# Values of the first self attention made for all heads at once, 512 columns at a time, and kept in the output buffer

## The chip, the core and the metric

The kernel runs on one core of a Trainium2 chip. The core has the engines TensorE (PE), VectorE (DVE), ScalarE (ACT) and GpSimd (POOL), and SyncE (SP), which issues the DMAs here. Each works through its own queue in order, and semaphores tie the queues together. SBUF holds the data, and PSUM, in eight banks of 128 partitions x 512 float32, takes what TensorE writes. The metric is the device time of one execution in microseconds (us).

## The reference, cut to what matters

Two decoder blocks run one after the other on x of shape (2, 1024, 256). The change touches only the first self attention of block 0 and the layer norm ahead of it:

```python
h = _layernorm(x, ln1_g, ln1_b)                # (2, 1024, 256)
q = (h @ wq).reshape(B, S, 16, 64)             # wq, wk, wv: 256 x 1024
k = (h @ wk).reshape(B, S, 16, 64)
v = (h @ wv).reshape(B, S, 16, 64)
attn = softmax(einsum('bihd,bjhd->bhij', q, k) * 64 ** -0.5)
out = einsum('bhij,bjhd->bihd', attn, v).reshape(B, S, 1024)
x = out @ wo + bo + x
```

All of it is float32. Cross attention, the gated feed forward layer and the whole of block 1 follow; they take the rest of the time and aren't touched.

## The kernel before

**Norm stage.** `project_norm` with the name ln01 normalises x in 9 groups of one or two tiles of 128 tokens. For each group DVE takes the statistics (`stats_of`) and ACT the root, DVE scales (`normalise`), PE transposes (`turn`), and ACT writes the transposed rows to hT, 128 partitions x 2 x 2048 (`evacuate`). A `Beside` object lets other work run in the slots of that loop; before the change only the split of the first weights into a coarse and a remaining part (`w_hi`, `w_lo`) runs there.

**Attention.** `wide_attention` handles two heads at a time (g = 0 to 7) for each of the two batches b: 16 bodies, `both(g, b)`. The code gives the first two bodies and the last two unrolled; the others are a hardware loop. A body has 8 units of two steps each. In a step, ACT seeds a score bank with the negative row maxima (`seed`), PE adds three products of the hi and lo parts of keys and queries (`scores`), ACT takes the exponential to `p_buf` (`exponent`), POOL adds `p_buf` up for the denominators, and PE multiplies `p_buf` with the values in `v_buf` (`weighted`).

Beside it each body prepares the next one, in "front items": the projections k and q of 512 tokens (6 matmuls each; ACT takes the hi part out of PSUM and DVE the lo part), the values v, sixteen m items (two products each for the row maxima, reduced by DVE), t (the transposed maxima, which DVE negates and SP sends through DRAM to `m_all`, from where the seeds come) and den (denominators). The tables `lanes` and `lanes_first` say in which unit of a body each item stands. In a unit PE does the items up to the first m (`leading`), the two steps of scores, the remaining items (`trailing`), and then the weighted products of the unit before. `first_front` is the list of items ahead of the first body, for which nothing else runs: I call this stretch the front.

All front items share three PSUM banks (`NBANK = 3`). An item takes the bank of its place in the `lanes` table, modulo 3 (an m item takes two places), whichever body it stands in, and PE's `wait_free` waits until the last user of that bank has been drained; for an m item it waits for both banks before the first product.

**Values before.** For each (g, b), items ("v", 0) and ("v", 1) each make the values of 512 tokens for the two heads at hand: 4 token tiles x 2 halves of the contraction, eight float32 matmuls of 128 columns (L1032), which PE runs as 16 passes; DVE copies the bank to `v_buf` (L1239). The weights `wv` of two heads are loaded for each g.

## Time and profile before

| | us |
|---|---|
| median of 3 runs | 1852.04 (1851.66 to 1856.6) |
| the profiled execution, device time | 1845.68 |
| its span, first to last instruction | 1844.0 |
| PE busy in the span | 1683.9 (91%) |
| DVE, ACT, POOL busy | 1179.0, 1057.4, 955.7 |
| const and norm stage, until the attention starts | 0 to 31.7 |
| front, until the first scores | 31.7 to 68.9 |
| first body, until the second body's scores | 68.9 to 127.4 |
| the other 15 bodies | 127.4 to about 786 |

The profile gives busy times by engine, and tables by line, by stretch and in order of time. "Idle before" an instruction is what its engine waited, with the engine that released it. Busy times of overlapping matmuls are not additive; what one costs is read from start to start.

### The profile page before, as it was taken

How to read it: one execution, taken by the hardware profiler on the slowest of the kernel's cores; microseconds unless marked ns; L12 is line 12 of the kernel's file. 1: busy time of each engine (PE TensorE's matmuls, PEld its weight loads, DVE VectorE, ACT ScalarE, POOL GpSimd, SP SyncE). 2: the span in 40 equal slices, each digit the busy share in tenths (PEclk: the TensorE clock that was granted, in tenths of full speed). 3: DMA queues.
4: the chain of work that ended last, by engine and by line, in shares of the span. 5: the costliest groups of instructions: out<-in, count | busy, mean ns of one | idle time of the engine just before them, and what ended most of it. 6: DMA issues, size and time to landing. Idle time of an engine off the chain costs nothing. (4 is left out here: it accounts for less than half of the span.)

```text
span 1844.0 us, 29564 instructions
## 1 busy us (share of the span) xinstructions
PE 1683.9 (91%) x10028; PEld 1079.8 (59%) x10028; DVE 1179.0 (64%) x2043; ACT 1057.4 (57%) x1389; POOL 955.7 (52%) x732
## 2 busy tenths in 40 slices
PE   4689999999999999988999889996989887998799
PEld 2345555555555555477666778884444436655679
DVE  5567777777776777475776843347787745787513
ACT  3367777787877787843555432311676673444452
POOL 1268888888888788951222620201334443566205
PEclk9899999999999999998999999996999999999899
DMA  2000100000000000030000010102334321000001
GB/s 83 18 26 30 36 32 26 29 26 29 26 29 26 29 26 24 24 103 27 1 1 1 13 32 23 30 12 62 76 71 105 72 71 30 10 1 7 26 17 47
DMA packets 53810, 62.46 MB, mean 34 GB/s; under 512 B 18064, under 2 KB 43820, under 8 KB 53711
## 3 DMA queue, kind: packets, MB, share of 16 engines
q1 hardware_dynamic: 53711, 61.16, 12.0%
q8 instruction: 60, 0.98, 0.2%
q14 instruction: 39, 0.32, 0.1%
HBM read 41.72 MB, written 2.37 MB: 24 GB/s over the span
## 5 line engine op out<-in xcount | busy, mean ns | idle before, releaser
L1336 POOL TENSOR_TENSOR x<-x,sa_p_buf 128x1024 f32<-128x1024 f32 x190 | 452.3, 2381 | 122.7 <-ACT sa_p_buf L1153 110.2
L1245 DVE TENSOR_REDUCE sa_mx<-sa_front 128x1 f32<-128x512 f32 x512 | 328.3, 683 | 113.3 <-PE sa_front L1041 112.3
L1153 ACT ACTIVATE sa_p_buf<-sa_score 128x1024 f32<-128x1024 f32 x256 | 248.9, 1023 | 130.2 <-PE sa_score L1078 130.2
L1093 PE MATMUL sa_out<-sa_p_buf,sa_v_buf 128*64 128x512 f32 x1024 | 246.2, 602 | 0.0
L607 ACT ACTIVATE sa_p_buf<-sa_score 128x1024 f32<-128x1024 f32 (+1 forms) x160 | 140.6, 943 | 76.0 <-PE sa_score L555 75.8
L402 DVE TENSOR_REDUCE sa_mx<-sa_front 128x1 f32<-128x512 f32 (+1 forms) x224 | 136.5, 651 | 31.5 <-PE sa_front L316 27.8
L1911 POOL TENSOR_TENSOR x<-x,bias_out 128x1024 f32<-128x1024 f32 x24 | 60.5, 2534 | 165.0 <-POOLq L2233 142.9
L1778 POOL TENSOR_TENSOR ca_probs<-ca_s_sb,ca_inv 128x616 f32<-128x616 f32 x64 | 78.0, 1219 | 120.5 <-DVE ca_inv L1694 120.5
L1093 PEld LDWEIGHTS sa_out<-sa_p_buf,sa_v_buf 128*64 128x64 f32 x1024 | 64.8, 136 | 120.2 <-issue 92.3
L1163 ACT ACTIVATE sa_score<-sa_m_all 128x1024 f32<-128x1024 f32 x128 | 130.7, 1033 | 6.1 <-DMA sa_m_all<-sa_m_line 6.1
L1041 PE MATMUL sa_front<-sa_k_hi,sa_q_hi 64*128 64x512 f32 x512 | 118.2, 458 | 12.4 <-DVE sa_mx L1245 6.6
L1163 ACT ACTIVATE sa_score<-x 128x1024 f32<-128x1024 f32 x128 | 127.8, 1031 | 2.6 <-DMA x<-sa_m_line 2.6
L660 POOL TENSOR_SCALAR_AFFINE_SELECT sa_p_buf<-sa_p_buf 128x128 f32<-128x128 f32 x256 | 65.7, 295 | 120.5 <-ACT sa_p_buf L607 120.5
L1267 DVE RECIPROCAL x<-x 128x128 f32<-128x128 f32 x124 | 108.7, 920 | 18.5 <-ACT x L1176 18.3
L1041 PEld LDWEIGHTS sa_front<-sa_k_hi,sa_q_hi 64*128 64x128 f32 x512 | 48.4, 185 | 113.1 <-DVE sa_mx L1245 38.2
L1601 ACT ACTIVATE ca_turned<-ca_t_ps 128x1024 f32<-128x1024 f32 x64 | 65.5, 1024 | 74.1 <-PE ca_t_ps L1547 74.1
L1078 PE MATMUL sa_score<-sa_q_hi,sa_k_hi 64*128 64x512 f32 x512 | 105.4, 408 | 2.7 <-ACT sa_score L1163 2.6
L1078 PE MATMUL sa_score<-sa_q_hi,sa_k_lo 64*128 64x512 f32 x512 | 101.1, 391 | 0.0
L1078 PE MATMUL sa_score<-sa_q_lo,sa_k_hi 64*128 64x512 f32 x512 | 100.7, 390 | 0.0
L1336 POOL TENSOR_TENSOR x<-sa_p_buf 128x1024 f32<-128x1024 f32 x32 | 75.9, 2372 | 46.2 <-ACT sa_p_buf L1153 46.2
L316 PE MATMUL sa_front<-sa_k_top,sa_q_top 33*128 33x128 f32 (+4 forms) x504 | 71.3, 349 | 23.8 <-DVE sa_mx L402 14.8
L316 PEld LDWEIGHTS sa_front<-sa_k_top,sa_q_top 33*128 33x128 f32 (+1 forms) x504 | 43.7, 193 | 78.0 <-DVE sa_mx L402 52.9
(238 smaller groups left out, 3587.9 us busy)
## 6 DMA issues: line engine op xcount, KB each, us to landing
sa_m_all<-sa_m_line SPq DMA_DIRECT2D x16, 512.0 KB, 3.6
x<-sa_m_line SPq DMA_DIRECT2D x16, 512.0 KB, 3.6
x<-in_x SPq DMA_DIRECT2D x8, 512.0 KB, 6.6
sa_q_stack<-sa_hi SPq DMA_DIRECT2D x32, 128.0 KB, 2.6
sa_k_stack<-sa_hi SPq DMA_DIRECT2D x32, 128.0 KB, 2.7
sa_recip<-sa_den_out SPq DMA_DIRECT2D x32, 128.0 KB, 2.6
ff_w<-in_L_xattn_ff_w SPq DMA_DIRECT2D x16, 128.0 KB, 2.2
sa_k_top<-sa_hi SPq DMA_DIRECT2D x32, 64.0 KB, 2.3
```

The costliest lines, as they stand in the source:

```text
L316: mm = pe.matmul(bank(i, item, u)[:, c0 + lo_k:c0 + hi_k], q_top[base:base + rows_of, b, r, at], k_top[base:base + rows_of, b, r, k0 + lo_ ...
L402: dve.tensor_reduce(mx[:, b, j, place:place + 1], fr[u][:, 0:n], AX.X, ALU.max).then_inc(drained, 1)
L607: nc.scalar.activation(p_buf[:, n % NPB, 2 * r:2 * r + 2, 0:cols], score_ps[r][:, :, 0:cols], ACT.Exp, scale=SCALE).then_inc(exp_done, 1)
L1041: pe.matmul(front_ps[bank(item, j)][:], q_hi[r, b, qt * P:(qt + 1) * P], k_hi[r, b, half * HALF:(half + 1) * HALF], start=True, stop=True) ...
L1078: mm = pe.matmul(score_ps[s % len(score_ps)][:, j, :], ks[r, b, keys], qs[r, b, queries], start=False, stop=(part == 2), skip_group_check= ...
L1093: mm = pe.matmul(out_ps[64 * j:64 * j + 64, :], v_buf[:, b, kt, 64 * j:64 * j + 64], p_buf[:, s % NPB, j, :], start=(kt == 0), stop=(kt == ...
L1153: nc.scalar.activation(p_buf[:, s % NPB], score_ps[s % len(score_ps)][:], ACT.Exp, scale=SCALE).then_inc(exp_done, G)
L1163: nc.scalar.activation(score_ps[s % len(score_ps)][:], m_all[h].rearrange("p (j n) -> p j n", j=G), ACT.Identity).then_inc(seeded, G)
L1245: dve.tensor_reduce(mx[:, b, j, qt, half:half + 1], front_ps[bank(item, j)][:], AX.X, ALU.max).then_inc(drained, 1)
L1267: dve.reciprocal(recip[:, h, at], recip[:, h, at]).then_inc(inverted, 1)
L1336: nc.gpsimd.tensor_tensor(acc[:, h], prev, cur, ALU.add).then_inc(added, 1)
L1778: nc.gpsimd.tensor_tensor(probs[:, n % 2, :, 0:TC], s_sb[:, n % NS], inv[:, n % 2, :].unsqueeze(2).to_broadcast((P, U, TC)), ALU.mult).the ...
```

## The change

The values of all sixteen heads are made once. Item n of 32 multiplies one tile of 128 tokens with 512 columns of wv, the columns of eight heads: two float32 matmuls of 512 columns. The result goes to the output buffer oT, into the places that the attention's own output takes later, and for each (g, b) one DMA brings 1024 columns of it to `v_buf`.

- Items 0 to 7 run in the norm stage (`AHEAD = 8`), in three PSUM banks of their own, one in each slot from 2 on; ACT takes them out.
- Items 8 to 17 (`IN_FRONT = 10`) run in the front, in the idle score banks, ACT takes them out.
- Items 18 to 31 stand in `lanes_first`, at the ends of the units of the first body (1, 1, 2, 2, 2, 2, 2, 2 of them), in the three front banks; DVE copies them (14 copies).
- The tables lose ("v", 0) and ("v", 1); q1 moves from unit 3 to 4, and in `first_front` behind t. A body has 40 places in place of 42.
- The front no longer primes the score banks with four products (L1101): the items 8 to 17 write them.
- All of wv, 1 MB, is loaded in the const stage, to the memory of the output weights `w_out`, whose own load moves from the start of the front to the second body. The loads of wq and wk for the first heads move from the norm stage to the const stage.
- The split of hT (`split_rows` on ACT, `rest_of_rows`) for batch 0 moves from the front into the norm stage, slots 4 and 6, with the lo part on POOL where DVE did it; that for batch 1 stands behind k1 in the front.
- In this norm stage, DVE takes the statistics of group i + 1 ahead of normalising group i.

```diff
+    def values(self, pe, n, ps):
+        half, tile = divmod(n, TT)
+        if n == 0:
+            pe.wait_ge(self.wv_in, DMA)
+        for k in range(KD):
+            mm = pe.matmul(ps, self.hT[:, k, tile * P:(tile + 1) * P], self.wv[:, k, half * HALF:(half + 1) * HALF],
+                           start=(k == 0), stop=(k == KD - 1))
+        return mm
...
+    def keep_values(self, act, n, ps):
+        act.wait_ge(self.v_full, n + 1)
+        self.nc.scalar.activation(self.values_to(n), ps.rearrange("p (g d) -> p g d", d=P),
+                                  ACT.Identity).then_inc(self.v_made, 1)
...
+    def tensor(self, pe, slot, ready):
+        n = slot - 2
+        if 0 <= n < self.AHEAD:
+            ready(n // GROUP)
+            if n >= len(self.early_ps):
+                pe.wait_ge(self.v_made, n - len(self.early_ps) + 1)
+            self.values(pe, n, self.early_ps[n % len(self.early_ps)][:]).then_inc(self.v_full, 1)
...
-        3: [("n", ("m", 2, 0)), ("n", ("m", 3, 0)), ("n", ("q", 1))],
-        4: [("n", ("m", 0, 1)), ("n", ("m", 1, 1)), ("n", ("v", 0))],
+        3: [("n", ("m", 2, 0)), ("n", ("m", 3, 0))],
+        4: [("n", ("m", 0, 1)), ("n", ("m", 1, 1)), ("n", ("q", 1))],
...
-        7: [("n", ("m", 6, 0)), ("n", ("m", 7, 0)), ("n", ("v", 1)), ("n", ("m", 4, 1))],
+        7: [("n", ("m", 6, 0)), ("n", ("m", 7, 0)), ("n", ("m", 4, 1))],
...
+    for u, count in enumerate((1, 1, 2, 2, 2, 2, 2, 2)):
+        lanes_first[u] = lanes_first[u] + [("c", ("v", n)) for n in in_lanes[:count]]
+        in_lanes = in_lanes[count:]
...
-    assert NSLOT % NBANK == 0
...
+                def load_values(g, b):
+                    sp.dma_start(v_buf[:, b], value_cols(g, b)).then_inc(v_in, DMA)
...
+                    if is_first(g, b):
+                        sp.wait_ge(v_made, TT)
+                    else:
+                        sp.wait_ge(pv_done, lin(g, b, STEPS, 0))
+                    load_values(g2, b2)
                     maxima(g2, b2, 0)
...
-                for c in range(HALVES, CHUNKS):
-                    pool.wait_ge(h_high, c + 1)
...
+                    first_w.rest_of_rows(pool, c)
...
+                if not KN:
+                    stats_of(0)
                 for i in range(NG):
-                    stats_of(i)
+                    if KN:
+                        stats_of(i)
+                    elif i + 1 < NG:
+                        stats_of(i + 1)
```

**PE in the front, between k1 and the fourth m item.** In the order of the kernel before, L1022 is a projection, L1101 the priming product and L1041 an m item. Before:

```order
L1022 MATMUL sa0_front2<-sa0_h_hi,sa0_w_lo 128x512
L1101 MATMUL sa0_score1<-hT,ident 128x512
L1041 MATMUL sa0_front1<-sa0_k_hi,sa0_q_hi 128x512 [waits sa0_drained]
L1041 MATMUL sa0_front2<-sa0_k_hi,sa0_q_hi 128x512
L1101 MATMUL sa0_score1<-hT,ident 128x512
L1041 MATMUL sa0_front0<-sa0_k_hi,sa0_q_hi 128x512 [waits sa0_drained]
L1041 MATMUL sa0_front1<-sa0_k_hi,sa0_q_hi 128x512
```

Now, with L1110, L764 (a value item) and L1126 for these:

```order
L1110 MATMUL sa0_front2<-sa0_h_hi,sa0_w_lo 128x512
L764 MATMUL sa0_score0<-w_out0,hT 128x512 x2
L1126 MATMUL sa0_front1<-sa0_k_hi,sa0_q_hi 128x512 [waits sa0_drained]
L1126 MATMUL sa0_front2<-sa0_k_hi,sa0_q_hi 128x512
L1126 MATMUL sa0_front0<-sa0_k_hi,sa0_q_hi 128x512 [waits sa0_drained]
L1126 MATMUL sa0_front1<-sa0_k_hi,sa0_q_hi 128x512
L764 MATMUL sa0_score0<-w_out0,hT 128x512 x2
```

A value item of two products stands ahead of every second m item.

**PE in unit 0 and 1 of the first body**, from the second m item of unit 0 to the first of unit 1. Before:

```order
L1041 MATMUL sa0_front0<-sa0_k_hi,sa0_q_hi 128x512 [waits sa0_drained]
L1041 MATMUL sa0_front1<-sa0_k_hi,sa0_q_hi 128x512
L1022 MATMUL sa0_front1<-sa0_h_hi,sa0_w_hi 128x512 [waits sa0_h_low_late,sa0_w_split,sa0_drained]
L1022 MATMUL sa0_front1<-sa0_h_lo,sa0_w_hi 128x512
L1022 MATMUL sa0_front1<-sa0_h_hi,sa0_w_lo 128x512
L1022 MATMUL sa0_front1<-sa0_h_hi,sa0_w_hi 128x512
L1022 MATMUL sa0_front1<-sa0_h_lo,sa0_w_hi 128x512
L1022 MATMUL sa0_front1<-sa0_h_hi,sa0_w_lo 128x512
L1041 MATMUL sa0_front2<-sa0_k_hi,sa0_q_hi 128x512 [waits sa0_drained]
L1041 MATMUL sa0_front0<-sa0_k_hi,sa0_q_hi 128x512
```

Now:

```order
L1126 MATMUL sa0_front2<-sa0_k_hi,sa0_q_hi 128x512 [waits sa0_drained]
L1126 MATMUL sa0_front0<-sa0_k_hi,sa0_q_hi 128x512
L1110 MATMUL sa0_front1<-sa0_h_hi,sa0_w_hi 128x512 [waits sa0_h_low,sa0_w_split,sa0_drained]
L1110 MATMUL sa0_front1<-sa0_h_lo,sa0_w_hi 128x512
L1110 MATMUL sa0_front1<-sa0_h_hi,sa0_w_lo 128x512
L1110 MATMUL sa0_front1<-sa0_h_hi,sa0_w_hi 128x512
L1110 MATMUL sa0_front1<-sa0_h_lo,sa0_w_hi 128x512
L1110 MATMUL sa0_front1<-sa0_h_hi,sa0_w_lo 128x512
L764 MATMUL sa0_front2<-w_out0,hT 128x512 [waits sa0_drained]
L764 MATMUL sa0_front2<-w_out0,hT 128x512
L1126 MATMUL sa0_front1<-sa0_k_hi,sa0_q_hi 128x512 [waits sa0_drained]
L1126 MATMUL sa0_front2<-sa0_k_hi,sa0_q_hi 128x512
```

The m item behind the projection took banks 2 and 0; it now takes 1 and 2, the banks of the projection and of the value item just ahead of it.

**PE in the last unit of a middle body**, from behind the scores to the weighted products. Before:

```order
L1041 MATMUL sa0_front1<-sa0_k_hi,sa0_q_hi 128x512 [waits sa0_drained]
L1041 MATMUL sa0_front2<-sa0_k_hi,sa0_q_hi 128x512
L1006 REGISTER_ALU
L1032 MATMUL sa0_front0<-sa0_wv,hT 128x128 [waits sa0_drained]
L1032 MATMUL sa0_front0<-sa0_wv,hT 128x128 x7
L1006 REGISTER_ALU
L1041 MATMUL sa0_front1<-sa0_k_hi,sa0_q_hi 128x512 [waits sa0_drained]
L1041 MATMUL sa0_front2<-sa0_k_hi,sa0_q_hi 128x512
```

Now:

```order
L1126 MATMUL sa0_front0<-sa0_k_hi,sa0_q_hi 128x512 [waits sa0_drained]
L1126 MATMUL sa0_front1<-sa0_k_hi,sa0_q_hi 128x512
L1097 REGISTER_ALU
L1126 MATMUL sa0_front2<-sa0_k_hi,sa0_q_hi 128x512 [waits sa0_drained]
L1126 MATMUL sa0_front0<-sa0_k_hi,sa0_q_hi 128x512
```

The second value item is gone, and the second of the two m items, now directly behind the first, shares bank 0 with it.

## Rows read from the trace of the kernel before

**Rows 1.** Busy time by stretch: stretch, length, busy us (count) by engine, PEclk, DMA, GB/s.
```profile
31.70:68.90 37.20, 23.18 (x85) 13.61 (x85) 17.84 (x28) 7.38 (x10) 4.97 (x2) 0.82 0.18 53
68.90:127.40 58.50, 45.50 (x256) 23.93 (x258) 34.11 (x55) 36.62 (x41) 32.24 (x15) 1.00 0.07 21
304.20:348.50 44.30, 44.30 (x262) 23.89 (x260) 31.57 (x50) 34.76 (x40) 36.87 (x18) 1.00 0.09 31
```

**Rows 2.** Groups by line: op, names, shapes, count, busy us, mean ns, idle.
```profile
L1032 PE MATMUL sa_front<-sa_wv,hT 128*128 128x128 f32 x512 | 65.6, 281 | 3.7 <-DVE sa_m_turned L1253 1.4 <-DVE sa_mx L1245 1.4 <-DVE sa_v_buf L1239 0.8
...
L1239 DVE COPY sa_v_buf<-sa_front 128x512 f32<-128x512 f32 x32 | 22.1, 692 | 27.0 <-PE sa_front L1032 27.0
```

**Rows 3.** PE's timeline in one middle body: start, duration, line, op, count.
```profile
321.48 0.51 PE L1041 MATMUL sa_front<-sa_k_hi,sa_q_hi 64*128 64x512 f32 x2
...
327.02 0.50 PE L1041 MATMUL sa_front<-sa_k_hi,sa_q_hi 64*128 64x512 f32 x2
...
329.06 2.05 PE L1032 MATMUL sa_front<-sa_wv,hT 128*128 128x128 f32 x16
...
332.91 0.50 PE L1041 MATMUL sa_front<-sa_k_hi,sa_q_hi 64*128 64x512 f32 x2
...
341.79 0.50 PE L1041 MATMUL sa_front<-sa_k_hi,sa_q_hi 64*128 64x512 f32 x2
...
344.19 2.05 PE L1032 MATMUL sa_front<-sa_wv,hT 128*128 128x128 f32 x16
...
348.47 0.50 PE L1041 MATMUL sa_front<-sa_k_hi,sa_q_hi 64*128 64x512 f32 x2
```

**Rows 4.** PE's timeline in the last body.
```profile
759.84 0.50 PE L1078 MATMUL sa_score<-sa_q_hi,sa_k_hi 64*128 64x512 f32 x2 [0.38 <-ACT sa_score L1163]
...
763.89 0.50 PE L1078 MATMUL sa_score<-sa_q_hi,sa_k_hi 64*128 64x512 f32 x2 [0.28 <-ACT sa_score L1163]
```

**Rows 5.** SP's timeline: the two weight loads issued in the first norm stage.
```profile
9.31 0.40 SPq L739 DMA_DIRECT2D sa_wqk<-in_L_xattn_sa_wq  x1
9.75 0.46 SPq L740 DMA_DIRECT2D sa_wqk<-in_L_xattn_sa_wk  x1
```

**Rows 6.** DVE's timeline in the first norm stage.
```profile
13.21 0.17 DVE L2041 RECIPROCAL ln_inverse<-ln_deviation 128x2 f32<-128x2 f32 x1 [0.27 <-ACT ln_deviation L2078]
```

**Rows 7.** ACT's timeline at the start of the attention's front.
```profile
31.67 3.90 ACT L1139 ACTIVATE sa_h_hi<-hT 128x1024 fp32r<-128x1024 f32 x4 [0.28 <-PEq L1883]
```

**Rows 8.** PE's timeline in the front.
```profile
34.13 0.76 PE L1022 MATMUL sa_front<-sa_h_hi,sa_w_hi 128*128 128x512 f32 x1 [3.59 <-DVE sa_h_lo L1221]
...
39.94 1.02 PE L1101 MATMUL sa_score<-hT,ident 128*128 128x512 f32 x2
40.40 0.80 PE L1022 MATMUL sa_front<-sa_h_hi,sa_w_hi 128*128 128x512 f32 x1
...
43.78 0.50 PE L1041 MATMUL sa_front<-sa_k_hi,sa_q_hi 64*128 64x512 f32 x2 [0.56 <-DVE sa_k_lo L1229]
...
47.15 0.50 PE L1041 MATMUL sa_front<-sa_k_hi,sa_q_hi 64*128 64x512 f32 x2 [1.38 <-DVE sa_mx L1245]
48.43 0.79 PE L1041 MATMUL sa_front<-sa_k_hi,sa_q_hi 64*128 64x512 f32 x2 [0.78 <-DVE sa_mx L1245]
...
58.09 0.80 PE L1022 MATMUL sa_front<-sa_h_hi,sa_w_hi 128*128 128x512 f32 x1 [1.37 <-DVE sa_mx L1245]
```

**Rows 9.** DVE's timeline at the end of the front.
```profile
62.30 0.27 DVE L1253 TENSOR_SCALAR sa_m_turned<-sa_front 8x128 f32<-8x128 f32 x1
```

**Rows 10.** ACT's timeline at the end of the front.
```profile
67.78 1.97 ACT L1163 ACTIVATE sa_score<-sa_m_all 128x1024 f32<-128x1024 f32 x2 [6.12 <-DMA sa_m_all<-sa_m_line]
```

**Rows 11.** PE's timeline in the first body, up to the second body's scores.
```profile
68.86 0.50 PE L1078 MATMUL sa_score<-sa_q_hi,sa_k_hi 64*128 64x512 f32 x2 [0.91 <-ACT sa_score L1163]
...
72.37 0.50 PE L1022 MATMUL sa_front<-sa_h_hi,sa_w_hi 128*128 128x512 f32 x1 [1.38 <-DVE sa_mx L1245]
...
127.41 0.40 PE L1078 MATMUL sa_score<-sa_q_hi,sa_k_hi 64*128 64x512 f32 x2
```

More of the change, by code:

```diff
@@ L815, in places @@
                     n += 1
-        order = [(0, item) for item in first_front]
+        prior = 0
+        for u in range(UNITS):
+            for _, item in lanes_first[u]:
+                if item[0] == "v":
+                    body[item, 0] = prior + 1
+                prior = body[item, 1 if item[0] == "m" else 0]
+        order = [(0, item) for item in first_front if item[0] != "v"]
         for i in range(2 * NG):
@@ L1064, in front_item @@
                     elif item[0] == "v":
[L1065 removed]
+                        values(item[1])
                     elif item[0] == "t":
@@ L1233, in front_item @@
                     kind = item[0]
+                    if kind == "v" and item[1] in IN_FRONT:
+                        return
                     fr = front_ps[bank(item)]
```

187 lines of the change are left out of this document (106 added, 81 removed), and 4 rows, old and new, of the table lanes_first.

## The prediction, made before the changed kernel had run

> **What bounds the kernel now.** I read the busy time by stretch first. In a middle body of the first self attention PE is busy for all of its 44.3 us at a granted clock of 1.00, while POOL has 36.9, ACT 34.8 and DVE 31.6 [rows 1]. So there time taken from PE counts, up to the point at which the order of small waits takes over. The first body and the front are another matter: PE is busy for 45.5 of 58.5 us and for 23.2 of 37.2 us, and the waits behind it name DVE draining front banks and the DMA of the maxima [rows 1, 8, 10, 11]. There extra PE work can partly hide, and a shorter chain counts. The table of groups by line then says what the values cost, and the timelines of PE, what stands beside them.
>
> **The steady bodies.** The old value products are 512 passes with 65.6 us of busy time, so 2.05 us for each of the 32 items [rows 2], the same as the 2.05 us of 16 passes in the timeline [rows 3]. Bodies 1 to 14 each lose two: 4.1 us. Body 15 prepares nothing and stays as it is. The priced removal would be 14 x 4.1 = 57.4 us. Against it stand waits that these items covered.
>
> In unit 7 the timeline has m, value, m. Now the two m items adjoin, and the second needs bank 0, in which the first has just put a product. The front shows that pattern with nothing between: PE waits 0.78 us for DVE's reduction in one form and 1.38 in the other, where the shared bank is the later one [rows 8]. Here it is the earlier one: 0.8 us.
>
> In unit 3, q1 leaves. The unit takes 327.02 - 321.48 = 5.54 us [rows 3], and a projection is six passes of 0.23, with its start about 1.6 us, so 3.9 would be left. Two units of the last body, which have scores and weighted products alone, take 763.89 - 759.84 = 4.05 us with PE waiting for ACT's seed [rows 4]. So unit 3 comes down on ACT's floor: 0.1 to 0.3 lost, and 0.2 more where q1 in unit 4 waits for the m item ahead. Unit 4 changes a value of 2.05 for q1. Together 1.3 us of new waits, a gain of 2.8 us per body, and 14 x 2.8 = 39.2 us. The bounds are 4.1 (no wait) and 2.0 (both m patterns at 1.38, and 0.7 in units 3 and 4).
>
> Who is next? At about 41.5 us per body POOL's 36.9 and ACT's 34.8 still fit; the exponentials lead POOL's additions by up to four buffers, so a lag of a unit costs nothing. The copies by DVE (0.69 us each [rows 2]) leave DVE too. The added DMA of 512 KB to `v_buf` is issued in unit 0 or 1 behind the wait for the last weighted products, and is wanted a body later. On SP it stands ahead of the next maxima, which are due only in unit 6. Nothing waits there: zero, as long as it lands within about 35 us; the DMA of 512 KB of maxima and the issue around it take 5.5 us [rows 9, 10].
>
> **The start.** SP now issues three more loads in the const stage, ahead of its last two stores. Two took 0.40 and 0.46 us [rows 5]; a third the same gives +1.4 us before the norm stage can start. In the norm stage DVE no longer waits for ACT's root: 0.27 us in nine groups [rows 6], -2.4. But PE gets eight value items and ACT eight evacuations of about 0.6 and two of the four splits that take 3.90 us together [rows 7]. PE's price of a value item: two products take 40.40 - 39.94 = 0.46 us for two passes, so 0.23 a pass [rows 8], four passes, 0.94 us; at the slower spacing that the engine had shortly before it would be 1.7. I take +2.0 for ACT's and PE's parts, so that the attention starts 1.0 us later than before.
>
> The split of the first rows is done by then. Before, PE's first projection came 2.5 us after ACT began with it (31.67 to 34.13 [rows 7, 8]); now it comes at about 33.0. From there to the first m item it took 9.65 us, in part at the slower spacing; I take 7.5, with a value item hidden behind the wait for k1's drain: 40.5 in place of 43.78. The m items follow in 13.5 us (two take 47.15 - 43.78 = 3.37 at the faster spacing [rows 8]); the value items stand in PE's wait of 1.38 ahead of every second one and cost nothing at 0.94. The turn of the maxima no longer stands behind q1 (58.09 to 62.30 before [rows 8, 9]), so DVE has them at 55.0 in place of 62.30. Another 5.5 us to the seed would be 60.5. PE, however, still has five value items and q1, 5 x 0.94 + 1.4 = 6.1 us, and ACT must evacuate the last before it seeds the same banks: 61.9. Before: 67.78 [rows 10]. The start gains 5.9 us. Bounds: a gain of 8 (no cost in the norm stage) and a loss of 5 (rival (b)).
>
> **The first body.** It gets 14 value items of 0.94 = 13.2 us, loses two of 2.05 and the waits of 1.4 around them (a wait of that kind: [rows 11]), in sum +7.7. On top come waits for banks just used, which the order shows: the m item ahead of unit 1 waits for the projection and the value item right ahead of it (a projection's bank is free about 3 us after its start, since ACT and then DVE read it), 2.1 us, and in unit 5 a value item waits for ACT to take the denominators, 0.8. I set +10.5 us, between 7 and 14.
>
> **Sum** for the profiled execution: -39.2 - 5.9 + 10.5 = -34.6 us on a span of 1844.0. The timed median lies 6.4 us above the profiled execution's 1845.68; I take the difference over unchanged: 1852.0 - 34.6 = 1817.4 us.
>
> **What a page would make of it.** The rows give 2.05 us for 16 passes of 128 columns, 0.128 each, and 0.23 for a pass of 512 [rows 2, 8]. The Trainium skill, "TensorE: Matmul & The Clock Gate", section "Back-to-back issue gap", gives about 81 ns and 131 ns for sustained streams with weight loads. By that an old item would cost 1.30 us and a new one 0.52, the gain per body would be 1.3 with the same waits, and the time about 1833. The trace disagrees at both widths, so I leave it 2 in 100.
>
> **Rivals.**
> (a) No new waits: the two m items find their banks free and unit 3 keeps its 3.9 us. Then 57.4 + 5.9 - 10.5 = 52.8 less, 1799. For it: DVE has 12 us to spare per body. Against it: the pattern of 0.78 in the front. 17 in 100.
> (b) The norm stage and the front run at the slower of the two clock levels (1.2 in place of 2.4 GHz). For it: the granted clock over the front was 0.82 on average [rows 1], and the first projections came in at the slow spacing after an idle of 3.59 us [rows 8]. A value item then costs 1.7: PE, not DVE, sets the pace of the norm stage (+4), and the six at the front's end and the projections take 7 us longer. The start is then about 5 us slower than before and the time 1828. Against it: PE now has work in all these gaps, and in the first body, busy 78%, it kept 1.00 [rows 1]. 13 in 100. The Trainium skill, same page, section "Part 1: The HAM clock gate", says that the clock follows how busy PE has lately been; by that the front would gain, as in my forecast.
> (c) Slower than before: the 40 places no longer divide by three banks, so that in every body neighbours meet in one bank, as in the first body, where such waits are 1.38 us each [rows 11]. The gain of 4.1 is used up by three of them per body; with four more than that, seven in all, a body takes 5.6 us longer, 14 x 5.6 = 78 us, with the start and the first body 83 us: 1935. From the order I see one such neighbour in a body (unit 7); at the seam of two bodies the weighted products lie between. 4 in 100.
> (d) The forecast's mechanism with dearer waits, 1.6 us gained per body and +14 in the first: 1838. 7 in 100.
>
> **How the numbers follow.** The forecast, 1809 to 1826, has 55 in 100; 2 are left for what I don't see. The range 1800 to 1830 takes in the forecast, (b) and about half of (a). A measurement can tell 0.3%, 5.6 us, from no change. Every case but (c) and some of the unseen is faster by more: faster 0.94, same 0.02, slower 0.04.
>
> **What would show it.** Middle bodies of 41.5 us with PE at 97% or more and waits of about 0.8 us ahead of the second m item of unit 7; unit 3 at 4.1; seed at about 62 and first body about 69 us long; value items of 0.94 us from start to start. I am wrong if the bodies differ from 41.5 by over 1 us, if ACT or POOL is what PE waits for in every unit, or if the first body grows by over 14 us.

## The result, and the profile after

The changed kernel takes 1827.61 us (median; 1825.43 to 1832.05), the kernel before, timed beside it, 1854.32: a ratio of 0.9882 (95% interval 0.9852 to 0.9913), 1.2% faster. Two later timings beside the kernel before gave 0.9912 (0.9881 to 0.9943) and 0.9879 (0.9859 to 0.9900). The forecast was 34.6 us less and a range that ended at 1830; the ratio times 1852.04 is 1830.2, just outside. The direction and the gain of the steady bodies were right, the start and the first body were wrong: the start lost where it was to gain, and the first body grew by 18.8 us, more than the 14 that the prediction gives as a sign of being wrong.

The profiled execution has a span of 1823.7 us (before: 1844.0). The changed kernel by stretch (the attention's front, its first body, a middle body), which answers to [rows 1]; columns as there:

```profile
40.38:74.82 34.44, 28.24 (x83) 13.25 (x83) 14.77 (x24) 11.22 (x18) 4.67 (x2) 1.00 0.12 39
74.82:152.16 77.34, 65.98 (x280) 30.50 (x282) 41.95 (x66) 36.66 (x41) 35.51 (x16) 1.00 0.06 21
317.99:359.42 41.43, 40.65 (x230) 20.06 (x228) 30.26 (x48) 34.77 (x40) 36.88 (x17) 1.00 0.13 44
```

A middle body fell from 44.25 to 41.43 us. The first body grew from 58.55 to 77.34, and the attention's first projection now comes at 40.38 in place of 34.13. The value items by form (out<-in, count, busy us, mean ns), which answer to [rows 2], and PE's timeline at the end of the front, which answers to [rows 8, 11]:

```profile
L764 PE MATMUL sa_front<-w_out,hT 128*128 128x512 f32 x56 | 26.0, 603 | 1.4 <-DVE sa_q_lo L1307 1.0 <-ACT x L1256 0.3
...
L764 PE MATMUL sa_score<-w_out,hT 128*128 128x512 f32 x40 | 18.7, 602 | 0.0
L764 PE MATMUL ln_front<-w_out,hT 128*128 128x512 f32 x32 | 17.2, 664 | 0.0
```

```profile
65.46 0.39 PE L1110 MATMUL sa_front<-sa_h_hi,sa_w_lo 128*128 128x512 f32 x1
65.69 7.03 PE L764 MATMUL sa_score<-w_out,hT 128*128 128x512 f32 x16
72.65 0.50 PE L1126 MATMUL sa_front<-sa_k_hi,sa_q_hi 64*128 64x512 f32 x2
74.82 0.50 PE L1164 MATMUL sa_score<-sa_q_hi,sa_k_hi 64*128 64x512 f32 x2 [1.67 <-ACT sa_score L1243]
```

Here the miss can be read at once. Sixteen value records of 512 columns run from 65.69 to 72.65: 0.435 us from start to start, 1.74 for an item of four. The projection's records ahead of them, just as wide, start every 0.23 us. What differs is the type: a projection multiplies fp32r operands, a value item float32 ones (the profile writes f32 for both). I had priced a value item by 0.23 a record.

DVE and POOL in the norm stage, and SP ahead of it, answer to [rows 5, 6]:

```profile
8.34 0.52 SPq L49 DMA_DIRECT2D sa_wqk<-in_L_xattn_sa_wq  x1
8.90 1.05 SPq L49 DMA_DIRECT2D sa_wqk<-in_L_xattn_sa_wk  x1
9.98 0.60 SPq L49 DMA_DIRECT2D w_out<-in_L_xattn_sa_wv  x1
```

```profile
11.78 0.75 DVE L2106 BATCH_NORM_STATS2 ln_stats<-x 128x6 f32<-128x256 f32 x2 [3.29 <-PEq L2406]
...
27.75 2.09 DVE L2124 TENSOR_SCALAR ln_normed<-x,ln_mean_var,ln_inverse 128x256 f32<-128x256 f32 x2
30.70 0.73 DVE L2124 TENSOR_SCALAR ln_normed<-x,ln_mean_var,ln_inverse 128x256 f32<-128x256 f32 x2
33.37 1.76 DVE L2124 TENSOR_SCALAR ln_normed<-x,ln_mean_var,ln_inverse 128x256 f32<-128x256 f32 x1
35.24 0.41 DVE L2124 TENSOR_SCALAR ln_normed<-x,ln_mean_var,ln_inverse 128x256 f32<-128x256 f32 x1
```

```profile
27.02 2.35 POOL L784 TENSOR_TENSOR sa_h_lo<-hT,sa_h_hi 128x1024 fp32r<-128x1024 f32 x1 [25.39 <-ACT sa_h_hi L779]
32.64 2.35 POOL L784 TENSOR_TENSOR sa_h_lo<-hT,sa_h_hi 128x1024 fp32r<-128x1024 f32 x1 [3.27 <-ACT sa_h_hi L779]
```

The three issues took 2.17 us, and DVE began at 11.78, about 2.3 us later than when they are issued in the norm stage (9.45, below). And two of DVE's normalisations took 2.09 and 1.76 us where the same form takes 0.73 and 0.41: both held instructions end just after the POOL subtraction that runs beside them (29.37 and 34.99).

PE's first item of the norm stage began at 17.94 and took 3.42 us from start to start, the second 2.12: the clock column begins with its first 1.00 at 23.0 us, and until then records start at half the pace.

**The ledger up to the last body.** Middle bodies: 14 of them, 619.64 us before, 580.19 after, -39.5 (39.45). First scores: 68.86 before, 74.82 after, +6.0. First body: +18.8. In sum the last body starts 14.7 us earlier (732.35 in place of 747.05). The other 5.6 us of the span's 20.3 come in later stages, whose code is the same.

### The profile page after: what moved, and what is told of

The parts are those of the page before. It is cut to its first block and busy times, and to the rows that moved or that the text cites. A ratio compares the mean times of both kernels' runs of the same rounds, so it can differ in the third digit from the quotient of the medians.

```text
span 1823.7 us, 28743 instructions
## 1 busy us (share of the span) xinstructions
PE 1666.9 (91%) x9636; PEld 1034.5 (57%) x9636; DVE 1167.3 (64%) x2023; ACT 1067.1 (59%) x1407; POOL 960.0 (53%) x734
## 5 line engine op out<-in xcount | busy, mean ns | idle before, releaser
L1233 ACT ACTIVATE sa_p_buf<-sa_score 128x1024 f32<-128x1024 f32 x256 | 249.2, 1024 | 116.6 <-PE sa_score L1164 116.6
L1126 PE MATMUL sa_front<-sa_k_hi,sa_q_hi 64*128 64x512 f32 x512 | 116.7, 451 | 19.1 <-DVE sa_mx L1325 15.6
L1126 PEld LDWEIGHTS sa_front<-sa_k_hi,sa_q_hi 64*128 64x128 f32 x512 | 48.0, 183 | 124.6 <-DVE sa_mx L1325 61.4
L1164 PE MATMUL sa_score<-sa_q_hi,sa_k_hi 64*128 64x512 f32 x512 | 108.2, 419 | 2.9 <-ACT sa_score L1243 2.9
L1677 ACT ACTIVATE ca_turned<-ca_t_ps 128x1024 f32<-128x1024 f32 x64 | 65.5, 1024 | 73.7 <-PE ca_t_ps L1623 73.7
L1164 PE MATMUL sa_score<-sa_q_hi,sa_k_lo 64*128 64x512 f32 x512 | 101.1, 390 | 0.0
L1164 PE MATMUL sa_score<-sa_q_lo,sa_k_hi 64*128 64x512 f32 x512 | 100.9, 390 | 0.0
```

The source lines that it names most:

```text
L1126: pe.matmul(front_ps[bank(item, j)][:], q_hi[r, b, qt * P:(qt + 1) * P], k_hi[r, b, half * HALF:(half + 1) * HALF], start=True, stop=True) ...
L1164: mm = pe.matmul(score_ps[s % len(score_ps)][:, j, :], ks[r, b, keys], qs[r, b, queries], start=False, stop=(part == 2), skip_group_check= ...
L1233: nc.scalar.activation(p_buf[:, s % NPB], score_ps[s % len(score_ps)][:], ACT.Exp, scale=SCALE).then_inc(exp_done, G)
```

## The experiments

The start of the first scores, of the second body and of the last body are read from PE's timeline (a row of L1164 in the changed kernel) in each trace. Three profiles of the changed kernel (the first, and the two below) give 74.82, 74.36 and 73.91 for the first scores; I compare with 74.4. Its first projection came at 40.38, 39.85 and 39.41; I compare with 39.9. These three follow the time at which the granted clock first rises in the norm stage, 23.0, 22.2 and 21.2 us: with a rise 1 us later the first projection comes about half a us later. Where no timing is given, a kernel ran once, and only its trace is read.

### The price of an item: whole, or half the contraction

Four kernels: the changed one again, and three in which items from a number on multiply half the contraction. The bound is 0 in one, 8 and 18 in the others. They leave out half of each such product, so their values are wrong, and only their time is read:

```
-        for k in range(KD):
+        parts = KD // 2 if n >= 0 else KD
+        for k in range(parts):
```

> The changed kernel, unaltered, as the base for the three others. Both theories expect 20 to 26 us less than the kernel before. What it can add: the trace of the first measurement had a further 5.6 us of difference in stages that the change doesn't touch. If that is chance, the part up to the last body's end is worth about -15 us here again and the later stages come out within 2 us of the kernel before.

> Every value item multiplies only the first half of the contraction (2 matmul records of 512 columns in place of 4), so the values are wrong; nothing else is changed. Theory P (the price: a float32 record of 512 columns takes PE 0.43 us, so an item 1.72 in place of my 0.94, and PE paces the norm stage, the end of the front and the first body): each item gets 0.87 us cheaper where PE sets the pace. Norm stage 3 to 5 us shorter, first scores another 4 to 6 us earlier (seed chain takes over), first body 77.3 -> 65 to 67 us; in all 20 to 24 us below the changed kernel. Theory W (waits: the item costs about 0.94, the rest are waits for drained banks, ACT's evacuations and the later start of the norm stage): at most 0.47 per item where PE sets the pace, 3 to 8 us in all.

> As the one with all items halved, but only items 8 to 31 (front and first body) are halved; the norm stage keeps whole items. Theory P: the norm stage stays as it is (attention starts at about 40.2), first scores at 69 to 71 in place of 74.8, first body 65 to 67; 15 to 18 us below the changed kernel. The 3 to 5 us between this and all halved are the norm stage's. Theory W: 3 to 7 us.

> Only the 14 items of the first body are halved. Theory P: first scores unchanged at 74.8, first body 77.3 - 14 x 0.87 = 65.1, or up to 67 if waits come up behind it; 10 to 12 us below the changed kernel. Theory W: the body is held by banks that DVE drains, and shrinks by under 4 us.

| kernel | first projection | first scores | first body | last body starts | timed (before 1845.35) |
|---|---|---|---|---|---|
| changed | 39.85 | 74.36 | 79.02 | 733.54 | 1827.8, 0.9912 |
| items 18 to 31 halved | 40.12 | 74.62 | 69.69 | 724.43 | 1817.9, 0.9852 |
| items 8 to 31 halved | 39.89 | 67.94 | 69.61 | 717.68 | 1817.9, 0.9855 |
| all halved | 37.10 | 66.46 | 71.29 | 717.88 | 1820.8, 0.9846 |

The price decides. Half an item costs PE 0.87 us, about the 0.94 that I had taken for a whole one, and with it the first body takes 69.69 us, where the forecast had 69.1. Each of these first bodies holds drops of the clock, told of below (one in the first three rows; 5.1 us in all in the last); without them the bodies would take about 77.3, 68.0, 67.9 and 66.2 us. In the front halving brings 6.4 us and in the norm stage 2.8 us at the first projection. Up to 1.2 of these 2.8 can be chance: the clock first rose at 19.8 us with all items halved, at 22.1 in the kernel that it is compared with. The theory of waits, at most 4 us in the body, falls. The theory of the price had sizes too large: it expected a first body of 65 to 67 us and 20 to 24 us in all. The saving in the body is 9.3 us and not the full 12.2; the likely reason, that part of an item's time lies in waits for banks that stay, wasn't tested. The timed medians don't follow the traces in the last two rows; the section on the clock says why.

With all items halved the first scores gain only 1.5 of the 2.8 us: the granted clock is 0.50 from 33.5 to 40.3, and PE's first projections start at the spacing of 0.43 us in place of 0.23.

### One cost at a time in the norm stage

First the loads, which SP issues in the norm stage again:

```
-                                                x_loads(x, x_dram, x_in) + first + first_w.first_loads())
+                                                x_loads(x, x_dram, x_in) + first)
...
+                        fetch_early(sp, first_w.first_loads())
```

> The changed kernel with the three loads of the first weights (wq, wk, wv) issued by SP in the norm stage again, behind which the norm stage's start doesn't wait. In the changed kernel their issues took 0.60, 0.95 and 0.61 us in the constants' stage, and DVE's first statistics came at 11.62 to 11.78 in place of 9.35. If the issues are the cause, DVE starts at 9.3 to 9.4 and the first scores come 2.0 to 2.3 us earlier, at 72.0 to 72.8. If PE's value items pace the stage whatever its start (they wait for wv, which now lands later), the start moves and the first scores gain under 1 us.

DVE began at 9.45, the first projection came at 38.34 and the first scores at 72.85: 2.2 us earlier at the start of the stage, 1.5 at the first projection and at the scores, just short of the expected 72.0 to 72.8. The issues are a cost of their own; where the other 0.7 us went wasn't followed.

Then the stage without PE's products. It leaves out the values of items 0 to 7; ACT copies from wv in their place:

```
-            self.values(pe, n, self.early_ps[n % len(self.early_ps)][:]).then_inc(self.v_full, 1)
...
-                self.keep_values(act, n, self.early_ps[n % len(self.early_ps)][:])
+                self.nc.scalar.activation(self.values_to(n), self.wv[:, 0, 0:HALF].rearrange("p (g d) -> p g d", d=P),
+                                          ACT.Identity).then_inc(self.v_made, 1)
```

> The changed kernel without PE's eight value items of the norm stage; ACT still makes its eight copies, from wv instead of from the products, so these values are wrong. Items 8 to 31 as they are. If the price of the float32 items is what lengthens the norm stage, the attention's first projection comes at 32.5 to 34.5 in place of 39.9 to 40.4 and the first scores 5.5 to 7.5 us earlier. If ACT's copies and splits, or the statistics, do it, the first projection stays above 38.

Neither theory as I had put it. The first projection came at 37.45, only 2.4 us earlier, and the first scores at 75.50, later than with the items. DVE's and POOL's rows (the first two views) show that POOL holds DVE, and PE's (the third), what an idle PE costs:

```profile
24.51 2.06 DVE L2113 TENSOR_SCALAR ln_var_eps<-ln_mean_var 128x2 f32<-128x2 f32 x1
...
31.43 1.73 DVE L2124 TENSOR_SCALAR ln_normed<-x,ln_mean_var,ln_inverse 128x256 f32<-128x256 f32 x1
```

```profile
24.20 2.34 POOL L784 TENSOR_TENSOR sa_h_lo<-hT,sa_h_hi 128x1024 fp32r<-128x1024 f32 x1 [22.57 <-ACT sa_h_hi L779]
30.66 2.35 POOL L784 TENSOR_TENSOR sa_h_lo<-hT,sa_h_hi 128x1024 fp32r<-128x1024 f32 x1 [4.12 <-ACT sa_h_hi L779]
```

```profile
37.45 0.77 PE L1110 MATMUL sa_front<-sa_h_hi,sa_w_hi 128*128 128x512 f32 x1 [3.03 <-PEq L1959]
38.02 0.63 PE L1110 MATMUL sa_front<-sa_h_lo,sa_w_hi 128*128 128x512 f32 x1
```

An addition on 128x2 elements takes 2.06 us in place of 0.17: POOL has just begun a subtraction, and both end together at about 26.55. That POOL is the cause is tested in the next section. And PE, busy for only 9 of 26 us of the norm stage, makes its projections at 0.43 us a record until 46.6; they and the m items take 26.0 us to the turned maxima, in place of 22.5.

And the kernel before with the new order of the statistics alone:

```
+                stats_of(0)
                 for i in range(NG):
-                    stats_of(i)
+                    if i + 1 < NG:
+                        stats_of(i + 1)
```

> The kernel before with one part of the change alone: DVE makes the statistics of a group one group ahead in the norm stage. I predicted 0.27 us in nine groups, 2.4 us: first projection at 31.7 in place of 34.1, first scores at 66.5 in place of 68.9. If the waits for ACT's root only change places, the gain is under 1 us. Bodies stay at 44.25.

The first projection came at 31.97, 2.16 us earlier (predicted 2.4), the first scores at 67.53, 1.3 earlier; in this front the granted clock stood at 0.50 for 17.1 us, in that of the kernel before for 13.7. That part does what I took it to do, where PE has nothing else in the stage.

### POOL's hold on DVE

```
     def gpsimd(self, pool, _):
+        pool.wait_ge(self.all_normed.sem, self.all_normed.since(9))
```

> The changed kernel with one edit: POOL begins its two subtractions for the low rows only when DVE has normalised all groups. In the runs so far DVE instructions that meet one of these subtractions (2.34 us each) end only after it: a normalisation of 0.73 us took 2.09, one of 0.41 took 1.76, and 4.18 where two POOL instructions stood in a row. If POOL holds DVE up (theory L), both normalisations fall back to 0.7 and 0.4 and the first projection comes at 38.0 to 38.7 in place of 39.9 to 40.4, the first scores 1.3 to 2.3 us earlier. If these durations are DVE's waits for PE or ACT, they stay, and the first projection comes at 40 or, as POOL is later, at 41.

All normalisations fell back to 0.73 and 0.41 us, and the first projection came at 38.30: theory L holds. But the first scores came at 74.04, since PE, idle for 2.2 us ahead of the projection, made it at a granted clock of 0.54, with 0.43 us from record to record:

```profile
36.00:38.30 2.30, 0.11 (x1) 1.00 0.00 0
38.30:42.00 3.70, 2.90 (x6) 0.54 0.35 142
42.00:46.00 4.00, 3.38 (x14) 1.00 0.02 4
```

(stretch, length, PE busy, PEclk, DMA, GB/s.) The Trainium skill says what this is: "SBUF — State Buffer", section "SBUF: two separate sides", has VectorE and GpSimd share a pair of ports under an exclusive lock, held for the whole instruction. By that, a DVE instruction that wants the pair waits until POOL's is done, however small it is. The traces agree: 2.06 us for 128x2 elements. In every trace in which a subtraction of POOL's ran beside the normalisations, each of DVE's scalings and additions that met it ended with it. Not every DVE instruction is held: the reciprocal on 128x1 elements at 33.17 in the changed kernel took 0.16 us while a subtraction ran (32.64 to 34.99).

### Items of fp32r parts

```
+            pairs = [(hs[:, k, rows], ws[:, k, cols]) for k in range(KD)
+                     for hs, ws in ((self.h_hi, self.wv_hi), (self.h_hi, self.wv_lo), (self.h_lo, self.wv_hi))]
```

for items 16 to 31, with wv's second half split by ACT and POOL in the norm stage.

> The changed kernel with items 16 to 31 (two in the front, the 14 of the first body) made of three products of split operands in fp32r, six records per item in place of four float32 records; ACT splits the second half of wv in the norm stage, POOL makes its low part. If the price is by type, 0.23 us for an fp32r record of 512 columns and 0.43 for a float32 one, an item takes 1.39 in place of 1.74: at most 14 x 0.35 = 4.9 us off the first body; by the share that halving brought (7.7 to 9.3 of 12.2 us) 3.2 to 3.8, a first body of 73.5 to 75.5. If a record of 512 columns costs 0.43 whatever its type, six make 2.6 us and the first body grows by 8 to 12 us.

The first body took 74.68 us, 73.0 without its one drop of the clock: 4.3 of the 4.9 us at most. So a record's price does go by type. The norm stage lost what this won, in part by the same hold: wv's subtraction and that of the low rows ran in a row, and each held one of two normalisations (4.18 us for the two, in place of 0.73):

```profile
25.10 4.18 DVE L2141 TENSOR_SCALAR ln_normed<-x,ln_mean_var,ln_inverse 128x256 f32<-128x256 f32 x2
```

```profile
24.37 2.35 POOL L829 TENSOR_TENSOR sa_wv_lo<-w_out,sa_wv_hi 128x1024 fp32r<-128x1024 f32 x1 [22.74 <-ACT sa_wv_hi L813]
26.80 2.34 POOL L796 TENSOR_TENSOR sa_h_lo<-hT,sa_h_hi 128x1024 fp32r<-128x1024 f32 x1
```

PE then waited 3.01 us for DVE, and its clock was 0.50 from 29.3 to 32.7, which costs up to 1.7 us more. The first projection came at 43.63.

### The order in the front, and the remedies together

```
-    first_front = [("k", 0), ("q", 0), ("k", 1), ("v", next(coming)), ("m", 0, 0), ("m", 1, 0), ("v", next(coming)),
+    first_front = [("k", 0), ("v", next(coming)), ("q", 0), ("k", 1), ("v", next(coming)), ("m", 0, 0), ("m", 1, 0), ("v", next(coming)),
...
-            return score_ps[n % NSCORE // G][:, n % G, :]
+            return score_ps[(n + 2) % NSCORE // G][:, n % G, :]
...
+                        if item == ("v", IN_FRONT.stop - 2):
+                            act.wait_ge(v_made, IN_FRONT.stop - 2)
+                            seed(0, 0, 0)
...
-                    seed(0, 0, 0)
```

> The changed kernel with two edits of order in the front: one value item stands between the first and the second projection, where PE waited 1.41 us for DVE, and ACT makes the first seed between the evacuations of the last four value items, whose banks are turned by two for it. Nothing is left out. If PE's work and this order set the start, the first scores come 1.4 and 1.7 us earlier, at 71.0 to 72.0. If ACT's or the DMA's chain behind the turned maxima sets it, under 1 us.

First scores at 70.96, 3.4 us earlier: as expected (71.0 to 72.0).

> The changed kernel with the three remedies together: loads issued in the norm stage, POOL behind the normalisations, and the two edits of order in the front. If each removes a cost of its own they add up: 1.5 to 2.0, 1.3 to 2.3 and 3.1 us, first scores at 67.0 to 68.5 in place of 74.4 to 74.8, first body as in the changed kernel (77.3, and 1.7 more for each dip of the clock); 5 to 8 us faster than the changed kernel, 0.983 to 0.987 of the kernel before. If PE's items only wait elsewhere, the gain is that of one of the three, 2 to 3 us.

> As the one before, and items 16 to 31 made of three fp32r products each, with wv's second half split by ACT and POOL in the front instead of in the norm stage. First scores 0.3 to 0.7 us earlier still, first body 4.3 us shorter (73.0 without a dip of the clock): 9 to 13 us faster than the changed kernel, 0.980 to 0.985 of the kernel before. If POOL's subtraction for wv holds up DVE in the front, as it did in the norm stage, the first scores come 1 to 2 us later than in the one before.

The first scores came at 69.99 and 69.56, 1.5 to 3 us later than expected for the one and 1.4 to 3.3 for the other. In both the granted clock fell at 38, half a us into the first projection, ahead of which PE had been idle (2.20 us in the first), and was 0.59 and 0.57 from 38 to 42, much as in the kernel with POOL's wait alone. The last body started at 729.51 and 723.13, 4 and 10 us earlier than in the changed kernel; timed, the two gave 0.9882 (0.9861 to 0.9902) and 0.9880 (0.9859 to 0.9900) of the kernel before, where 0.983 to 0.987 and 0.980 to 0.985 were expected: no more than the changed kernel itself.

The first of these two still had POOL at work until 36.9, and the first projection came at 37.41. So in the next two POOL's second subtraction was moved behind the norm stage:

```
-        for c in range(2):
-            self.rest_of_rows(pool, c)
+        self.rest_of_rows(pool, 0)
...
-                for c in range(HALVES, CHUNKS):
+                for c in range(1, CHUNKS):
```

> The changed kernel unaltered, beside the two that follow on the same chip. By the trace of every kernel so far, the part behind the last body (its code is the same in all) takes 1055 us and as much more as its stretches at a lower granted clock give away: 1089 to 1106 us between executions. If that rule holds, the profile here has again 1055 +- 2 us plus that loss. Timed 0.986 to 0.992 of the kernel before.

> As the kernel with the three remedies (float32 items), with POOL's second subtraction of low rows moved out of the norm stage, whose end waited for it (POOL ended at 36.9, the attention began at 37.4 with PE idle for 2.2 us and then 1.5 us lost at a lower clock). If that end was the wait, the first projection comes at 36.0 to 36.6, without the drop of the clock the first scores come at 67.2 to 68.2 in place of 70.0; 5 to 9 us faster than the changed kernel before the later stages' chance of +-8. If PE falls to the lower clock all the same, 69.

> The same with items 16 to 31 of fp32r parts. First scores 66.8 to 68, first body 73.4, last body's start 720 to 721.5 in place of 732.4 to 733.5: 11 to 13 us faster than the changed kernel up to there. Timed 4 to 16 us faster, since the later stages' clock adds up to 8 us either way; 0.979 to 0.986 of the kernel before.

| kernel | first projection | first scores | first body | last body starts | timed (before 1847.55) |
|---|---|---|---|---|---|
| changed | 39.41 | 73.91 | 80.74 | 734.74 | 1826.28, 0.9879 (0.9859 to 0.9900) |
| remedies, float32 | 35.83 | 66.79 | 79.49 | 726.38 | 1820.87, 0.9856 (0.9829 to 0.9882) |
| remedies, fp32r parts | 37.04 | 67.32 | 73.45 | 720.89 | 1823.92, 0.9884 (0.9856 to 0.9912) |

With the clock at 1.00 ahead of the projections the first scores come 7.1 us earlier than in the changed kernel of the same call. Up to the last body the two kernels are 8.4 and 13.9 us faster; 1.7 and 3.4 of this are drops of the clock in the first body, of which the changed kernel has two here, the first of the others one and the second none. Timed, the first is 5.4 us faster by its median, with intervals that overlap; of the second, for which 4 to 16 us were expected, no gain can be told. The last section of the experiments has a measure that can tell it. That the second's first projection comes 1.2 us later than the first's goes with a clock that first rose at 22.1 us in place of 19.7.

### The steady body

> The changed kernel with the second q projection put back from unit 4 to unit 3, in all bodies, so that unit 3 keeps its old items and unit 4 loses a value item without getting anything. Theory: a unit without items for PE comes down to ACT's 3.9 us and no further. Unit 3 goes back to 5.5, unit 4 falls from 5.85 to 3.9 to 4.1, and a body takes 41.1 to 41.3 in place of 41.43. Rival: the projection's 1.6 us were hidden in unit 4 behind waits for drained banks; then unit 4 falls by under 1 us and a body takes 42 us.

The first scores of units 2 to 5 of a middle body, with q1 in unit 3:

```profile
330.13 0.40 PE L1164 MATMUL sa_score<-sa_q_hi,sa_k_hi 64*128 64x512 f32 x2
...
335.62 0.40 PE L1164 MATMUL sa_score<-sa_q_hi,sa_k_hi 64*128 64x512 f32 x2
...
341.12 0.40 PE L1164 MATMUL sa_score<-sa_q_hi,sa_k_hi 64*128 64x512 f32 x2
...
345.04 0.49 PE L1164 MATMUL sa_score<-sa_q_hi,sa_k_hi 64*128 64x512 f32 x2
```

Unit 3 takes 341.12 - 335.62 = 5.50 us and unit 4 3.92, the times that I expected. But the theory behind them doesn't hold: it is not ACT that ends such a unit. Unit 3 of the changed kernel, with the same work for PE (stretch, length, then PE, weight loads, DVE, ACT and POOL, PEclk, DMA, GB/s):

```profile
335.20:339.11 3.91, 3.91 (x26) 1.80 (x23) 3.38 (x6) 2.92 (x4) 3.28 (x2) 1.00 0.00 0
```

PE is busy for all of it, with no wait in its rows, and ACT for 2.92 us, with a wait of 1.21 for PE's scores. So 3.91 is what PE needs for two m items, two steps of scores and the weighted products, and no floor of ACT's was reached. A body still takes 41.42 us, since unit 5 went from 4.98 to 5.33. My 41.1 to 41.3 was wrong. In that unit ACT is busy for 5.30 us of the 5.33 (4.46 of 4.99 in the changed kernel), so ACT's work is the likely limit there; it wasn't tested. For the change it doesn't matter in which of the two units q1 stands.

### The clock and the later stages

Why do medians not follow the traces? The part from the last body's start on has the same code in all kernels, yet it took from 1089 to 1106 us. I summed (1 - PEclk) x 20 us over all windows of 20 us from 700 to 1840:

| kernel | from the last body's start to the end | lost to the clock | difference |
|---|---|---|---|
| before, first profile | 1097.0 | 41.4 | 1055.6 |
| changed, first profile | 1091.4 | 36.4 | 1055.0 |
| changed, second | 1089.3 | 33.0 | 1056.3 |
| all items halved | 1105.8 | 50.2 | 1055.6 |
| first remedies, parts | 1104.1 | 49.2 | 1054.9 |
| last remedies, float32 | 1090.6 | 34.8 | 1055.8 |
| last remedies, parts | 1097.2 | 45.8 | 1051.4 |

In all 18 profiles the difference lies between 1051.4 and 1056.3. The expectation of 1055 +- 2 was made from the first 14; of the last four profiles three hold it. So nearly all of the difference between the kernels in this part is what a lower granted clock gives away, in some executions at places where in others it stays. The last two kernels of the table (stretch, length, PE busy, PEclk, DMA, GB/s), float32 first, then parts:

```profile
1440.00:1480.00 40.00, 33.27 (x294) 1.00 0.30 68
1480.00:1520.00 40.00, 31.59 (x227) 1.00 0.26 62
1520.00:1560.00 40.00, 32.30 (x165) 0.96 0.05 11
```

```profile
1440.00:1480.00 40.00, 33.76 (x296) 0.96 0.30 74
1480.00:1520.00 40.00, 33.10 (x211) 0.96 0.18 49
1520.00:1560.00 40.00, 32.42 (x157) 0.91 0.05 11
```

Of the 5.6 us that the first comparison gained in unchanged stages, 5.0 are this. The mean clock is on record for every timed execution, and settles more than the seven profiles do. Span times mean clock, lowest to highest:

| kernel | executions | span x mean clock, us |
|---|---|---|
| changed, first call | 4 | 1783.2 to 1788.2 |
| items 18 to 31 halved | 4 | 1775.3 to 1778.0 |
| items 8 to 31 halved | 4 | 1768.2 to 1771.0 |
| all halved | 4 | 1761.2 to 1769.3 |
| changed, last call | 5 | 1784.0 to 1788.4 |
| last remedies, float32 | 5 | 1779.0 to 1781.9 |
| last remedies, parts | 6 | 1769.0 to 1776.7 |

By this measure the last remedies stand apart from the changed kernel in every execution, by 5.9 and 13.0 us at the median (6.7 and 10.5 by the traces up to the last body, drops in the first body taken off), and halving in the front shows where the timed medians were equal. So at an equal clock both remedies are faster, and a lower clock in the later stages took most of the second one's gain back.

What decides where it falls stays open: of the five profiles whose last body starts earliest four lost 42 to 50 us, but so did the kernel before with its statistics moved (44.8, last body at 745), the first with parts (46.4, at 732) and the one with the new order in the front (44.4, at 732).

The same happens in the first body. In the first profile of the changed kernel the clock stayed at 1.00; in the one beside the last remedies it fell twice, each time costing about 1.7 us (units 4 and 5: 13.29 and 12.93 in place of 11.66 and 11.24):

```profile
112.00:117.00 5.00, 2.84 (x21) 0.98 0.00 0
117.00:120.40 3.40, 3.40 (x8) 0.53 0.00 0
120.40:129.00 8.60, 7.22 (x33) 1.00 0.01 2
129.00:134.00 5.00, 4.73 (x11) 0.66 0.00 0
```

Ahead of the first fall PE was busy for 2.84 of 5 us, waiting for banks.

## Why the prediction was right in part and wrong in part

**Right: the steady bodies.** -39.2 predicted, -39.5 measured. Unit 3 lost 1.62 us and stands at 3.91 (forecast 4.1 by ACT's floor, which wasn't reached: PE is busy throughout); unit 4 lost 0.04 (forecast 0.25); unit 7 lost 1.14 (forecast 1.25), the value item's 2.05 less a new wait, which the trace shows between the two m items:

```profile
355.60 0.40 PE L1126 MATMUL sa_front<-sa_k_hi,sa_q_hi 64*128 64x512 f32 x2
356.78 0.49 PE L1126 MATMUL sa_front<-sa_k_hi,sa_q_hi 64*128 64x512 f32 x2 [0.78 <-DVE sa_mx L1325]
357.20 1.94 PE L1179 MATMUL sa_out<-sa_p_buf,sa_v_buf 128*64 128x512 f32 x8
```

The 0.78 is the front's number [rows 8] that I took for it. That the sum came out within 0.3 us is in part luck: unit 3 gave 0.2 us more than forecast, units 4 and 7 0.3 less. The load of `v_buf` delayed nothing: from 160 to 700 us PE's only listed waits are those for DVE's maxima, 13 of them, 10.2 us.

**Wrong: the price of a value item**, 0.94 us for a measured 1.74. This is the step that failed, and it is in two terms of the sum: the first body's 14 x 0.94 = 13.2 us, and the start, where it is in the norm stage's +2.0, in the items that were to fit into PE's waits of 1.38, and in the five at the end, 5 x 0.94. I took it from the start of the next row, 40.40 - 39.94 [rows 8]. But the two records of L1101 multiply float32, and the row behind them is an fp32r record that was already queued: its duration of 0.80 us, in place of 0.40, holds its wait for them. The rows of the second record and of the one after that in the kernel before are

```profile
40.37 0.59 PE L1101 MATMUL sa_score<-hT,ident 128*128 128x512 f32 x1
...
41.03 0.40 PE L1022 MATMUL sa_front<-sa_h_lo,sa_w_hi 128*128 128x512 f32 x1
```

The second starts 0.43 us behind the first, at 40.37. And 41.03 less the 0.23 of the record at 40.40 leaves 40.80 - 39.94 = 0.86 us for the two, 0.43 each. [rows 2] could have warned: 0.128 us for 128 columns would be 0.51 for 512, and I took less than half of that. The work in columns didn't change, so PE saves little in all: the float32 products cost 65.6 us before and 32 x 1.74 = 56 after. The gain is that they left the steady bodies, where PE is busy all the time, for stages in which a part of them fits into waits. The Trainium skill has the reason in "FP8 and Floating Point Precision", section "TensorE Precision Notes": true FP32 takes four passes through the array. The trace shows two records per float32 matmul and 0.435 us for each, so 0.87 against 0.23 for the fp32r matmul, close to four.

**Wrong: the start**, -5.9 predicted, +6.0 measured. By steps: the first projection came at 40.4 in place of my 33.0, 7.4 us later. Issuing the loads in the norm stage brought 1.5 us of it back (1.4 was in the forecast, for a cost of 2.3), POOL's wait alone 1.6 (its hold is 2.7 us by the rows above), and both, with POOL's second subtraction moved out, 4.1 (39.9 to 35.8). PE's price is up to 2.8 (halving all against halving from item 8 on: 39.89 - 37.10). These were measured each with other costs in place, so they needn't add up; that 4.1 and 2.8 come near 7.4 is an estimate of the shares and no proof of them. From there to the first m item took 7.7 us (7.5 predicted), from the first m item until DVE has the maxima 14.7 (14.5), and from there to the first scores 12.0, where the forecast had 8.0. These 4.0 us are five items at 1.74 in place of 0.94: the price again. The first body: +18.8 in place of +10.5; 9.3 of it went when its items were halved, which leaves +9.5, near what I had predicted for the whole.

**The rivals.** None is what happened. (a) expected no new waits, and there is the one of 0.78. (b), a slower clock in the norm stage and the front, had nearly the time (1828), for another reason: in the first profile the clock was 1.00 from 40 to 150, and only PE's first two items, until 23.0 us, were made at the slow spacing. The front even gained here: in the kernel before, the granted clock in it was 0.50 from 48.1 to 61.7. Where PE had no items in the norm stage, the slow projections of (b) did come, which fits what I had put against it, that PE's new work keeps them away. (c) expected bodies longer than before, and they are shorter. (d) had dearer waits; the waits were right and the work was dearer. The rule of the Trainium skill ("TensorE: Matmul & The Clock Gate", section "Back-to-back issue gap"), 1833 by the prediction's estimate, came near too, but by bodies of 43 us, where the trace has 41.43.

**Not foreseen at all:** POOL's hold on DVE. The change took two subtractions of low rows, those of batch 0, from DVE in the front and gave them to POOL in the norm stage, where DVE's scalings read SBUF. The prediction counts ACT's and PE's parts of the norm stage and leaves POOL's out.

**The range** ended at 1830. An item at 1.7 us was named in the prediction as the price at the slower spacing, and went into rival (b) alone, for the norm stage and the front; the first body's bound of 14 leaves no room for it. With the 2.8, 4.0 and 9.3 us above the sum is -34.6 + 16.1 = -18.5, or 1833.5, outside the range.

## What to carry to other kernels

Read the price of a record from a long run of its own kind, start to start, and never from the start of the row behind it: in these traces a queued matmul of another type gets its start 0.4 us too early, and shows it by a duration of 0.80 us, twice its usual. Where work moves onto an idle POOL, look at which of DVE's instructions will run beside it. And before work is spread into a stage to fill an engine's gaps, look at its clock: the fill can pay for a part of itself by keeping the clock up, and a shortcut that leaves PE idle for 2 us can lose its gain.

## What the runs showed of the hardware

- A float32 matmul of 512 columns is two records of 0.435 us, an fp32r one is one record of 0.23 us. With three fp32r products in place of each float32 product, the six records of an item take 1.39 us, where the four float32 records take 1.74.
- POOL's tensor_tensor of 128x1024 elements (2.34 us) holds DVE's tensor_scalar on SBUF, even one on 128x2 elements (2.06 us in place of 0.17), until it is done; two in a row held one of two scalings each, 4.18 us in place of 0.73. Reciprocals and aggregates on 128x1 and 128x2 elements in SBUF ran beside it in their usual 0.15 to 0.18 us. DVE's reductions from PSUM aren't held: four took 2.57 us beside POOL's subtractions (48.08 to 52.75) and 2.56 without, later in the front.
- The granted clock in the profile reads 1.00 for the first projections of the kernel with no PE items in the norm stage, although their records start every 0.43 us in place of 0.23, until 46.6 us. The Trainium skill, "TensorE: Matmul & The Clock Gate", section "What's actually happening", has PE idle at 1.2 GHz by default, and the spacing fits that; the column shows a lower clock only from its first change on, as far as these traces go.
- A drop of the clock in the first body cost about 1.7 us each time; in the later stages the clock lost gives 33 to 50 us of 1140 in the profiles, and equal code took up to 16 us more in one execution than in another.
